# A two-layer mixture-of-experts kernel: second layer's experts of groups 0 to 2 on rows sorted by expert

## The reference, cut to what matters

```python
xn = _layernorm(x)
x = x + _L0_attn_ref(xn, ...) + _L0_ffn_ref(xn, ...)     # scan; 8 experts, dense
xn = _layernorm(x)
x = x + _L1_attn_ref(xn, ...) + _L1_ffn_ref(xn, ...)     # r, k, v, o; 8 experts, top 2

def _L0_ffn_ref(...):                                    # E = 8, F = 256
    weights = _router_weights(x, Wr, temperature)
    mid = jax.nn.silu(gate) * up                         # 256 -> 256 per expert (LoRA on two)
    out = jnp.einsum('ebtf,efd->ebtd', mid, Wd)
    return jnp.einsum('bte,ebtd->btd', weights, out)

def _L1_ffn_ref(x, gate_w, expert_w, expert_b):          # E = 8, TOPK = 2
    logits = jnp.einsum('td,ed->te', xf, gate_w)
    top_w, top_i = jax.lax.top_k(logits, TOPK)
    top_w = jax.nn.softmax(top_w)
    gates = zeros.at[arange(T)[:, None], top_i].set(top_w)
    y = jnp.einsum('td,edo->eto', xf, expert_w) + expert_b[:, None, :]
    return jnp.einsum('te,eto->to', gates, y)
```

## Time and profile before

| | us |
|---|---|
| median of three runs | 481.67 |
| profiled execution, device time | 483.39 |
| its span, first to last instruction | 481.6 |
| TensorE busy | 469.2 (97%) |
| DVE busy | 378.5 (79%) |
| ACT busy | 145.1 (30%) |
| POOL busy | 95.9 (20%) |
| one middle group (260.34 to 372.24) | 111.90 |

### The profile page before, as it was taken

How to read it: one execution, slowest core, us unless ns; L and a number is a source line. 1 busy time by engine, 2 the same in 40 slices (tenths; PEclk the granted TensorE clock), 3 DMA queues, 4 the chain that set the end, 5 groups by cost and what they waited for, 6 DMA issues and landing times.

```text
span 481.6 us, 7341 instructions
## 1 busy us (share of the span) xinstructions
PE 469.2 (97%) x2684; PEld 410.8 (85%) x2684; DVE 378.5 (79%) x1139; ACT 145.1 (30%) x283; POOL 95.9 (20%) x104
## 2 busy tenths in 40 slices
PE   8989999899999999999999999999999999999997
PEld 5778898788878898898888998898888898999886
DVE  6988698788996648877898756869899755768896
ACT  5345456512021333323030323342112222333020
POOL 3415579710070002400010000420002000400002
PEclk9997999989999999998999999999999999999999
DMA  8981000000001100000001000000000100000001
GB/s 280 302 360 44 2 1 1 1 1 1 1 1 44 45 1 1 0 2 2 0 0 45 17 29 1 0 2 0 1 1 1 45 0 1 1 2 1 2 0 44
DMA packets 7251, 15.45 MB, mean 32 GB/s; under 512 B 856, under 2 KB 5232, under 8 KB 6576
## 3 DMA queue, kind: packets, MB, share of 16 engines
q1 hardware_dynamic: 5168, 13.13, 7.9%
q10 hardware_dynamic: 2048, 1.86, 1.2%
HBM read 12.89 MB, written 2.10 MB: 31 GB/s over the span
## 4 chain that ended last, share of the span: by engine, by line
PE 74%; DVE 10%; issue 9%; POOL 4%; ACT 1%; DMA 1%; SPq 0%; DVEq 0%; POOLq 0%
PE G L459 22%; PE U L459 21%; PE D L459 20%; PE M L459 7%; DVE mid_lo L1000 1%; POOL w_lo L381 1%; DMA w_raw<-weights 1%; PE M L489 1%; DVE acc L1132 1%; PE M L468 1%; PE M L605 1%; DVE xT_lo L1000 1%; DVE mid L1118 1%; POOL acc L420 1%; DVE stats L1200 1%
## 5 line engine op out<-in xcount | busy, mean ns | idle before, releaser
L459 PE MATMUL D<-w_hi,mid_hi 128*128 128x256 f32 x288 | 83.9, 291 | 4.2 <-DVE acc L1132 4.1
L459 PE MATMUL D<-w_hi,mid_lo 128*128 128x256 f32 x288 | 83.3, 289 | 0.0
L459 PE MATMUL D<-w_lo,mid_hi 128*128 128x256 f32 x288 | 83.2, 289 | 0.0
L1118 DVE TENSOR_TENSOR mid<-mid,U 128x512 f32<-128x512 f32 x58 | 39.4, 685 | 49.3 <-PE U L459 44.9
L798 ACT ACTIVATE mid<-G 128x512 f32<-128x512 f32 x58 | 34.3, 596 | 124.1 <-PE G L459 123.1
L459 PEld LDWEIGHTS D<-w_hi,mid_hi 128*128 128x128 f32 x288 | 57.0, 198 | 6.8 <-issue 5.4
L381 POOL TENSOR_TENSOR w_lo<-w_raw,w_hi 128x512 fp32r<-128x512 f32 x35 | 48.2, 1406 | 65.1 <-DVE shift_g L1287 25.1
L459 PEld LDWEIGHTS D<-w_lo,mid_hi 128*128 128x128 f32 x288 | 57.0, 198 | 0.8
L459 PEld LDWEIGHTS D<-w_hi,mid_lo 128*128 128x128 f32 x288 | 56.9, 198 | 0.0
L1000 DVE TENSOR_TENSOR mid_lo<-mid,mid_hi 128x512 fp32r<-128x512 f32 (+1 forms) x70 | 52.6, 763 | 5.1 <-ACT mid_hi L771 2.4
L771 ACT ACTIVATE mid_hi<-mid 128x512 fp32r<-128x512 f32 (+1 forms) x70 | 41.2, 592 | 43.7 <-DVE mid L1118 39.1
(11 more groups left out here) (252 smaller groups left out, 963.3 us busy)
## 6 DMA issues: line engine op xcount, KB each, us to landing
w_raw<-weights SPq DMA_DIRECT2D x5, 1024.0 KB, 18.4
w_raw<-weights SPq DMA_DIRECT2D x3, 768.0 KB, 12.6
out<-ln SPq DMA_DIRECT2D x16, 128.0 KB, 1.8
xres<-x ACTq DMA_DIRECT2D x7, 256.0 KB, 3.0
w_raw<-weights SPq DMA_DIRECT2D x4, 256.0 KB, 5.9
w_raw<-weights SPq DMA_DIRECT2D x2, 512.0 KB, 7.7
gu_factors<-lora_gu SPq DMA_DIRECT2D x2, 256.0 KB, 11.7
xres<-x SPq DMA_DIRECT2D x1, 256.0 KB, 2.9
```

Source lines behind the costliest of these rows:

```text
L459: ins = nc.tensor.matmul(out_ap, a, b, start=(first and n == 0), stop=(last and n == 3 * len(pairs) - 1))
L1118: v.tensor_tensor(mid[:, c, :], mid[:, c, :], GU[2 * c + 1][:, :], ALU.mult)\
```

## The change

The layer-1 experts of groups 0 to 2 (1536 rows, two experts each, 3072 rows in all) are no longer computed densely. Per group, after the gates:

- POOL counts the chosen experts of each tile (`count_chosen`), TensorE ranks each row among its expert's rows by two matmuls of 40 columns (`rank`), DVE turns ranks into row numbers (`find_places`). ACT writes each normalised row twice, once per chosen expert, each scaled by its gate (`weigh`); POOL scatters the rows, 128 at a time, into a DRAM area with a region per expert (`scatter`, eight indirect DMAs a group).
- SP clears both DRAM areas (two of 12,416 rows of 1 KB) with zeros before.
- The output projection, the gate transposes and the attention's moments of a group move into experts 1 to 3 of the next group, where also `route_best` now stands. Partial results of groups 0 and 1 go to DRAM.
- In the last group a table of 31 blocks of 128 sorted rows (blocks of an expert are filled up with zeros; 3072/128 + 7 = 31 always suffice) gives each block its expert and its place. Two blocks make a unit. SP loads a unit's rows, TensorE transposes them (`unit_transpose`), ACT and DVE make high and low parts, TensorE multiplies by the expert's weights, whose address is in a register (`unit_product`), ACT copies out, SP stores. Units 0 to 7 stand among experts 6 and 7, the others behind.
- At the end POOL gathers each row's two results with 24 indirect DMAs that add in flight (`gather`), and SP stores the tiles of groups 0 to 2.
- Group 3's layer-1 experts stay dense; its experts 5 to 7 are no longer halved. High and low parts of the layer-1 expert weights are made in group 1 instead of group 0. `acc` and `xres` become one tile, `rows`, of which there are two.

```diff
-SCAN_AT = (5, 3, 3, 3)
+LAST = GROUPS - 1
+SCAN_AT = (5, 4, 4, 4)
...
+REGION = LAST * GT
+PIECES = 2 * LAST * GT // P + E - 1
+UNITS = (PIECES + 1) // 2
+UNIT_TILES = [range(2 * u, min(2 * u + 2, PIECES)) for u in range(UNITS)]
...
-HIGH_BY = (7, 10, 16, 21, 26, 32, 35, MATS)
+FIRST_MATS = WHERE["expert0"]
...
@@ SP @@
+            def clear(dram, zeros):
+                for e in range(E + 1):
+                    empty = dram[e * REGION:min((e + 1) * REGION, E * REGION + P), :].rearrange("(n p) d -> p n d", p=P)
+                    sp.dma_start(empty, zeros.broadcast_to([P, empty.shape[1], D])).then_inc(cleared, 16)
+            sp.wait_ge(zero_made, 1)
+            clear(sorted_rows, weighted[0][:, 0:1, :])
+            clear(expert_rows, weighted[0][:, 0:1, :])
...
+            def load_unit(u):
+                if u >= STAGES:
+                    sp.wait_ge(unit_T_ps, u - STAGES + 1)
+                for i, n in enumerate(UNIT_TILES[u]):
+                    sp.dma_start(stage[u % STAGES][:, i, :], sorted_rows[bass.ds(at_row[n], P), :])\
+                        .then_inc(sorted_loaded[u % STAGES], 16)
+            def store_unit(u):
+                sp.wait_ge(unit_evicted, u + 1)
+                for i, n in enumerate(UNIT_TILES[u]):
+                    sp.dma_start(expert_rows[bass.ds(at_row[n], P), :], made[u % RINGS][:, i, :])\
+                        .then_inc(made_stored[u % RINGS], 16)
...
+            for u in range(STAGES):
+                load_unit(u)
+            for u in range(UNITS):
+                store_unit(u)
+                if u + STAGES < UNITS:
+                    load_unit(u + STAGES)
+                if u == UNITS // 2:
+                    sp.wait_ge(gu_ps, at(LAST, 4 * E, 20))
+                    for g in range(2):
+                        sp.dma_start(sums_of[g], part[g * GT:(g + 1) * GT, :].rearrange("(t p) d -> p t d", p=P))\
+                            .then_inc(part_loaded, 16)
+            for n in range(LAST * TILES):
+                sp.wait_ge(summed[n], 32)
+                sp.dma_start(out[n * P:(n + 1) * P, :], sums_of[n // TILES][:, n % TILES, :]).then_inc(stored, 16)
+            sp.wait_ge(stored, 16 * TILES * GROUPS)
 
@@ POOL @@
+            def count_chosen(g):
+                pool.wait_ge(gap_ready, g + 1)
+                nc.gpsimd.memset(chosen_ahead[:, 0, :], 0.0)
+                nc.gpsimd.memset(chosen[:, TILES, :], 0.0)
+                steps(nc.gpsimd.tensor_tensor(chosen[:, 0:TILES, :], hot[:, :, 0, :], hot[:, :, 1, :], ALU.add))
+                steps(nc.gpsimd.tensor_copy(chosen_ahead[:, 1, :], chosen[:, 0, :]))
+                for t in range(1, TILES):
+                    steps(nc.gpsimd.tensor_tensor(chosen_ahead[:, t + 1, :], chosen_ahead[:, t, :], chosen[:, t, :],
+                                                  ALU.add))
...
+            def scatter(g):
+                pool.wait_ge(cleared, 16 * 2 * (E + 1))
+                pool.wait_ge(slots_ready, g + 1)
+                for t in range(TILES):
+                    for j in range(2):
+                        pool.wait_ge(weighted_ready, at(g, 2 * TILES, 2 * t + j + 1))
+                        q = g * TILES + t
+                        nc.gpsimd.indirect_dma_start(sorted_rows[:, :],
+                                                     bass.IndirectOffsetOnAxis(slots[:, q, j:j + 1], 0),
+                                                     weighted[j][:, t, :], None).then_inc(scattered, 16)
+            def gather(n, j):
+                if j == 0:
+                    if n < 2 * TILES:
+                        pool.wait_ge(part_loaded, 16 * 2)
+                    else:
+                        pool.wait_ge(result_ready, at(LAST - 1, TILES, n % TILES + 1))
+                else:
+                    pool.wait_ge(summed[n], 16)
+                nc.gpsimd.indirect_dma_start(sums_of[n // TILES][:, n % TILES, :], None, expert_rows[:, :],
+                                             bass.IndirectOffsetOnAxis(slots[:, n, j:j + 1], 0),
+                                             compute_op=ALU.add).then_inc(summed[n], 16)
 
             for g in range(GROUPS):
...
                     add_beta(1)
+                if g < LAST:
+                    count_chosen(g)
+                    scatter(g)
+                    if g == LAST - 1:
+                        pool.wait_ge(gu_ps, at(LAST, 4 * E, 4))
+                        nc.gpsimd.iota(tile_id, pattern=[[1, 32]], base=0, channel_multiplier=0,
+                                       allow_small_or_imprecise_dtypes=True).then_inc(ids_made, 1)
+                    att_low(g)
+                    if g == 0:
+                        split_low(FIRST_MATS, MATS)
+            for n in range(RINGS):
+                pool.wait_ge(made_stored[n], 16 * sum(len(UNIT_TILES[u]) for u in range(UNITS) if u % RINGS == n))
+            for n in range(LAST * TILES):
+                gather(n, 0)
+            for n in range(LAST * TILES):
+                if n == 4:
+                    att_low(LAST)
+                gather(n, 1)
 
@@ TensorE @@
+            def rank(g):
+                pe.wait_ge(bias_made, 5)
+                pe.wait_ge(chosen_step, at(g, TILES + 1, TILES + 1))
+                seen = M0[:, 0:(TILES + 1) * E]
+                nc.tensor.matmul(seen, mean_w, chosen_ahead.rearrange("p t e -> p (t e)"), start=True, stop=False)
+                nc.tensor.matmul(seen, ahead, chosen.rearrange("p t e -> p (t e)"), start=False, stop=True)\
+                    .then_inc(rank_ps, 1)
+            def unit_transpose(u):
+                bank = unit_banks(u)[0]
+                pe.wait_ge(sorted_loaded[u % STAGES],
+                           16 * sum(len(UNIT_TILES[n]) for n in range(u % STAGES, u + 1, STAGES)))
+                if u:
+                    pe.wait_ge(unit_lo_ready, u)
+                for i in range(len(UNIT_TILES[u])):
+                    for k in range(KC):
+                        ins = nc.tensor.transpose(bank[:, (2 * k + i) * P:(2 * k + i + 1) * P],
+                                                  stage[u % STAGES][:, i, k * P:(k + 1) * P], ident[:, :])
+                ins.then_inc(unit_T_ps, 1)
+            def unit_product(u, owners):
+                bank = unit_banks(u)[1]
+                pe.wait_ge(unit_lo_ready, u + 1)
+                if u:
+                    pe.wait_ge(unit_evicted, u)
+                for i, n in enumerate(UNIT_TILES[u]):
+                    ins = passes(bank[:, i * D:(i + 1) * D],
+                                 [(pieceT_hi[u % 2][:, k, i, :], pieceT_lo[u % 2][:, k, i, :],
+                                   w_hi[:, bass.ds(owners[n], 1), k, :].rearrange("p a d -> p (a d)"),
+                                   w_lo[:, bass.ds(owners[n], 1), k, :].rearrange("p a d -> p (a d)"))
+                                  for k in range(KC)])
+                ins.then_inc(unit_ps, 1)
 
...
+            def unit(u, owners):
+                unit_transpose(u)
+                if u:
+                    unit_product(u - 1, owners)
             def group(g, nxt):
+                for e in range(1, E):
+                    if g == LAST and e == 6:
+                        need(f"expert{E - 1}")
+                        pe.wait_ge(table_ready, 1)
+                        pe.wait_ge(scan_normed, at(g, TILES, TILES))
+                        _, owners = nc.values_load_multi_w_load_instructions(
+                            owner_at[:, 0:PIECES], engines=[nc.tensor.engine], min_val=WHERE["expert0"],
+                            max_val=WHERE["expert0"] + E - 1,
+                            skip_runtime_bounds_check_because="the table holds the number of one of the experts")
+                    gate_up(g, e, [0])
+                    if g and e == 2:
+                        moments(g - 1, 1)
...
+                    early = UNITS - LATE_UNITS
+                    for u in range(8, early):
+                        unit(u, owners)
+                    unit_product(early - 1, owners)
+                    pe.wait_ge(unit_evicted, early)
+                    transpose_y(g)
+                    pe.wait_ge(silu_ready, at(g, 2 * E, 2 * E))
+                    pe.wait_ge(mid_ready, at(g, 2 * E, 2 * E))
+                    for u in range(early, UNITS):
+                        unit_transpose(u)
+                        if u > early:
+                            unit_product(u - 1, owners)
+                    unit_product(UNITS - 1, owners)
                     pe.wait_ge(yT_lo_ready, at(g, KC, KC))
+                    pe.wait_ge(down_added, at(g, 2 * E, 2 * E))
                     project_rkv_half(g, 0)
@@ ACT @@
+            def weigh(g, tiles):
+                act.wait_ge(row_gain_ready, g + 1)
+                act.wait_ge(cleared, 16 * 2 * (E + 1))
+                act.wait_ge(scattered, at(g, 16 * 2 * TILES, 0))
+                for t in tiles:
+                    for j in range(2):
```

(62 more changed lines are left out.)

655 lines of the change are left out of this document (341 added, 314 removed).

## The result

The changed kernel takes 513.6 us in the median of its runs beside 481.9 for the kernel before: a ratio of **1.065**, 95% interval 1.058 to 1.072, so it is slower. In a second set of runs it took 514.0, ratio 1.064 (1.059 to 1.069). The profiled execution took 511.4 with a span of 509.5, that is 27.9 more than the span of before, and the medians differ by 31.7; the prediction's sum was +26.8, its forecast 508.

What follows compares the result with a forecast made beforehand. TensorE, busy 97% of the span, was taken to bound the kernel. Terms of 6.1 (with -30.6 removed net), 6.7, 4, 5 and 5 summed to +26.8 us, added to the median 481.67: 508 us, range 476 to 532.

Steps and rivals of the forecast that it cites:

- Removed and added on TensorE, -30.6: TensorE overall: 65.3 us of dense expert products go, 34.7 of block matmuls, transposes and rank matmuls come; net -30.6 us.
- Crossings, +19.5: Previous group's pieces inside the next group's experts, three times: TensorE waits of 1.3, 2.8 and 2.4 us, 6.5 each time.
- middle groups of 97 us: Sign that the forecast is right: middle groups take 97 us, not 111.9.
- POOL's queue in group 1, +7.6: Group 1's end: expert weights' low parts stand ahead of POOL's scan addition, so TensorE waits 7.6 us for DVE.
- The scan's wait and the loads, +3.3 and +4: Last group: TensorE waits 3.3 us for normalised scan rows before expert 6; 31 register loads behind that cost 4.
- The halved experts' own waits: Last group: its last experts are no longer halved, and their own waits go with that, some -2.5 us.
- Register addresses, +5: Units' 186 matmuls with addresses in registers: 0 us if hidden in the 0.12 step, 22 if not; 5 taken.
- the rival built on it: TensorE's sequencer: register loads of 0.6 us one by one and 0.1 us an address give 536 us; chance 0.08.
- Zeros, 0: Clearing the DRAM areas, 25.4 MB: ends near 119 us, before ACT's weighted copies at 128; costs nothing.
- Clock, +5: TensorE's clock: three more half-clock dips of 3.4 us, each losing 1.7; 5 us taken, between 0 and 14.
- Gathers' tail, +6.7: Kernel's end: POOL's 24 gathers at 1.3 us each end 6.7 us after TensorE's own path; between +0.3 and +43.
- The rival in which POOL ends the kernel: Kernel's end: at 2.3 us a gather POOL's tail costs +27 instead of +6.7, 528 us in all; chance 0.12.

Runs made afterwards that it cites:

- Experiments 3: Changed kernel with the second moments product, gate transposes, output projection and related DVE pieces one step later in each crossing: 496.8 us, ratio 1.031.
- 4: Changed kernel with the end of the first layer's routing left out in groups 1 to 3, which take group 0's weights: 498.4 us, ratio 1.033.
- 7: Kernel before the change, with the 48 second-layer expert products of groups 0 to 2 and DVE's 96 sums left out, nothing in their place: 472.7 us, ratio 0.980.
- experiment 5: Changed kernel with the second twelve of the 24 gathers left out: 498.1 us, ratio 1.031.
- experiment 1: Changed kernel with POOL's low parts of the expert weights in group 1 behind its scan additions instead of in front: 510.7 us, ratio 1.060.
- experiment 10: Changed kernel with several reorderings (485.2 us), further edited so the first twelve gathers are plain copies into a buffer that DVE adds: 486.9 us, ratio 1.003.
- experiment 2: Changed kernel with TensorE's 31 register loads ahead of its scan wait, and that wait behind expert 6's first gate/up products: 506.0 us, ratio 1.046.

## Why the prediction was right, and which terms were not

The direction and the mechanism hold: less work on TensorE, given back by orders on the other queues. The measured 513.6 lies well inside the range of 476 to 532, which is wide. By its steps, predicted against measured:

- **Removed and added on TensorE, -30.6.** The products' step is 0.12 as forecast. The unit's transposes were priced too high: four of them start 0.11 apart (0.45 us for four in the chain at 428.14) and not 0.176, where the eight of the earlier trace rows wait for DVE tile by tile. That is 6.8 us for 62, not 10.9. SP issues 62 block loads and stores, not 124; the 1.8 us a unit is for four of them and stands.
- **Crossings, +19.5.** Measured 18.0, with the releasers named: 1.3, 2.8, 2.4 were forecast, 1.0 to 1.3, 2.4 to 2.6 and 2.4 came. Experiments 3 and 4 confirm DVE's order; 7 shows that the walk was worth its length, as the same chain left in its old order costs 47.9. The sign "middle groups of 97 us" did not come: the third stretch, which had 113.5, has 100.7, with 6.1 of waits and two half-clock stretches in it.
- **POOL's queue in group 1, +7.6.** 7.3, with POOL's additions at the root.
- **Last group.** The scan's wait and the loads, +3.3 and +4, came as 6.1 in one piece. The halved experts' own waits were not measured by themselves. From the end of down(7) to the last product the trace has 26.1 us, the walk 26.6.
- **Register addresses, +5.** Nothing: the twelve matmuls of a unit take 1.70 us in the chain, a first step of 0.21, ten of 0.12 and the last one's 0.28, and a matmul without registers has the same longer first step. The trace of before could not tell this; the rival built on it falls.
- **Zeros, 0.** Nothing, as said above.
- **Clock, +5.** The waits of before that I read as 2.1 to 2.4 us are 2.0 and 2.1 (4.1 together). I counted three more dips. Eight half-clock stretches stand against three, 28.9 us against 11.5: 8.7 lost. Six of the eight stand in or within 2 us behind a wait of about 2.4 us or more. That is no rule: each crossing has two such waits, and the second, 2.4 us ahead of the output projection, is followed by none; the experiments that removed most waits also removed some of them. Where they fall differs from kernel to kernel, also in stretches that an edit does not touch, and the unedited kernel in its second set of runs has its first at 50 us, not at 38. So an effect of 2 or 3 us in one execution is not read from its span.
- **Gathers' tail, +6.7.** This is the term that was most wrong. TensorE's path would have ended 39.6 us behind the last product at 454.1, at 493.7 (with half of the gathers it ends 40.1 behind, experiment 5); the span ends at 509.5, so the tail is 15.8. I took 1.3 us a gather, like POOL's own instructions; it is about 1.55 and 0.30 of issue, 1.85, so that the first sixteen end 33.9 us behind the last product and not ahead of attention's high parts, which come 28.7 behind it. Also, my sum was wrong: 30.6, two low parts (2.6), 10.4, 3 and 2.3 are 48.9 and not 46.3, so the term by its own pieces was +9.3. The bounds, 0.45 and 3.0, hold it. The rival in which POOL ends the kernel was right in kind and had a dearer gather (2.3): the case between it and the forecast came.

The errors nearly cancel: 4.1, 5, 1.5 and 1.2 too high, 9.1 and 3.7 too low, one more us in all. That 26.8 met the 27.9 of the two profiled spans is luck, and by the medians it is 31.7. The prediction's total is better than its terms.

What stays open: whether moving POOL's low parts alone (experiment 1) gains anything, what brings on the half-clock stretch at 212 us, which stands behind no wait (the one at 38 stands behind one of 2.0), and what held DVE in experiment 10. No kernel was run without the zeros, so DMA traffic as a rival is answered by the trace alone.

## What to carry to other kernels

Work on the bound engine that is removed is worth what is left after the chain that it covered: find that chain, engine by engine, before counting columns; here taking out 65 us of products, with nothing put in their place, gained 9. Then walk each queue in its order. A piece that is asked for one step before its input is ready costs that wait in every pass, and moving it one step later gave 17 us without touching any work.

## What the runs showed of the hardware that I had not expected

- A gather that adds holds POOL 1.54 to 1.58 us, one that copies 0.95, a scatter 0.98, each for 128 rows of 1 KB, and 0.30 pass between two. The addition costs 0.6 us of POOL's time.
- 31 register loads on TensorE leave 0.8 us without a matmul when matmuls are queued ahead of them and 3.1 behind a wait (experiment 2). Matmuls with register addresses keep the 0.12 us step.
- Beside POOL's low parts (SBUF to SBUF, 1.24 us each) DVE's smallest operations take 1.19 us, not 0.16 (experiment 1).
